# TensorE's table reads stand singly between the gate/up products; the find products move to the last step of four

## The chip, the cores and the metric

The kernel runs on one core of one Trainium2 chip. The metric is the device time of one execution in microseconds (us). Engines are named as in the profile: PE is TensorE's matmul side, PEld its weight loads, DVE VectorE, ACT ScalarE, POOL GpSimd, SP SyncE. A name with a q behind it (PEldq, DVEq, SPq) is that engine's sequencer: the part that reads the instruction stream, works on registers, checks semaphores and hands work to the engine.

## The reference

A state space layer (layer norm, a four-tap convolution, a scan, two projections, residual) is followed by a mixture of experts over 8192 tokens of 512 numbers. Only the second half meets the change:

```python
topk_w, topk_idx = _route(x, w_router, b_router)      # 8 of 64 experts per token
sort = jnp.argsort(idx_flat); tok = sort // TOPK      # (token, expert) pairs by expert
g = jax.lax.ragged_dot(x_sorted, we_gate, group_sizes)   # 512 -> 256
u = jax.lax.ragged_dot(x_sorted, we_up, group_sizes)
o = jax.lax.ragged_dot(jax.nn.silu(g) * u, we_down, group_sizes)   # 256 -> 512
y = jnp.zeros_like(x_flat).at[tok].add(o * w_sorted[:, None])
```

The data type is float32 throughout.

## The kernel before, in words

The stages up to the routing end some 917 us after the span's start. The rest is `expert_tiles`, and only it is touched. It goes over 576 tiles of 128 (token, expert) pairs. 65,536 pairs fill 512 tiles; the other 64 are room for the partly filled last tile of each expert, and those that the routing leaves over stand at the end and carry no token.

A table row in on-chip memory (`k.tiles`, three words a tile) says for each tile which expert it has, whether that expert is new, which of four weight slots it uses, and which earlier tile's result must have been added before its own may be. An engine that needs the word reads it into a register: `entry` is a `value_load`, and `Words.load` keeps the word and its slot number. On every engine these reads have the line 1301 in the profile.

Each product is made of three passes over weights and data split into a high and a low fp32r part. For a tile TensorE does, in this order inside `step(i, s)`:

- `turn_x(i + 1)`: four transposes of the next tile's gathered rows (line 1407), into `ps_x`. It needs `xT_low` of tile i, since the same PSUM tile is used again.
- `find` (line 1420), once in four steps: four small products that compare `past` with the ranks of an expert's tokens, for four tiles that come 12 tiles later. It needs the expert number of each as a register.
- `gate_up(i)`: twelve products of 128x128 by 512 columns (line 1438).
- `turn_h(i - 1)`: two transposes of the hidden row (line 1465).
- `down(i - 2)`: six products (line 1455).

`walk` unrolls the loop eight times, so s runs from 0 to 7; registers don't live across a turn of the loop, so step s = 0 loads the words of tiles i-2, i-1 and i anew. Each later step has the word of its tile from the step before, where `words.load(i + 1, s + 1)` stands right behind the gate/up products. Once in four steps (s of 0 and 4) `experts_of` reads four more entries there, for the four find products of the next step.

VectorE goes over the same tiles in groups of four (`short_walk`). In its step it makes `xT_low` of tile i+1 (`keep_low`, line 1578), splits the weights of a new expert (`split_low`, line 1570: 2.34 us for the gate/up part, 1.23 us for the down part), takes or prepares the find's results, then makes `h` (`hidden`, line 1590), `hT_low` (line 1584) and `y` (`scale`, line 1597). `mark` (line 1602) writes `past`, the comparison that a find multiplies with; `pick` (lines 1609 to 1618) turns two tiles' find results into token numbers, `tile_ids`. ScalarE copies them out seven tiles ahead (`take_ids`, line 1535), and GpSimd gathers the rows five tiles ahead (line 1373). GpSimd also adds the scaled results into the output in memory (line 1381), after SyncE has counted the earlier ones as landed (line 1351); for a tile that carries no token the table asks for all tiles before it.

Of the kernel before, what the change touches and what calls it, by code (L numbers as in the profile page):

```python
# [20 lines left out]
E, F, TOPK = 64, 256, 8  # L21
# [1176 lines left out]
def expert_tiles(nc, k):  # L1198
# [8 lines left out]
    with ExitStack() as ctx:  # L1207
# [92 lines left out]
        def entry(eng, i, field, most):  # L1300
            return eng.value_load(k.tiles[0:1, bass.ds(3 * i + field, 1)], min_val=min(field, 1),  # L1301
                                  max_val=most)
# [95 lines left out]
        @block.tensor  # L1398
        def _(pe):
            words = Words(pe)  # L1400

            def turn_x(i, s):
                pe.wait_ge(gathered[s % XS], 16 // XS * (i - s % XS) + 16)
                after(pe, xT_low_ready, i)
                chunks = x[:, s % XS, 0:D].rearrange("p (q c) -> p c q", c=DC)
                for c in range(DC):
                    last = nc.tensor.transpose(ps_x[:, c, :], chunks[:, c, :], k.ident[:])  # L1407
                last.then_inc(xt_done, 1)

            def experts_of(i):  # L1410
                return [pe.snap(entry(pe, i + t, 0, 2 * WSLOTS * E - 1) // (2 * WSLOTS), min_val=0, max_val=E - 1)
                        for t in range(SHORT)]

            def find(i, experts):


                pe.wait_ge(marked, i + SHORT)
                after(pe, picked, i)
                for t, e in enumerate(experts):
                    last = nc.tensor.matmul(ps_find[t // 2][:, t % 2, :], past[:, t, :],  # L1420
                                            k.ranks[:, bass.ds(e, 1), :].rearrange("j o t -> j (o t)"), start=True,
                                            stop=True)
                    if t % 2 == 1:
                        last.then_inc(found, 2)

            def gate_up(i, s):
                place = words.place(s)
                high, low = (w[:, bass.ds(place, 1), 0:DOWN].rearrange("p o (j c f) -> p c (o j) f", j=2, c=DC)
                             for w in (w_high, w_low))
                pe.wait_ge(w_low_ready[0], i + 1)  # L1430
                pe.wait_ge(xT_high_ready, i + 1)
                after(pe, h_made, i - 1)
                n = 0
                for x, w in ((xT_high, high), (xT_high, low), (xT_low, high)):
                    if x is xT_low:
                        pe.wait_ge(xT_low_ready, i + 1)
                    for c in range(DC):
                        last = nc.tensor.matmul(ps_gu[s % 2][:], x[:, s % 2, c, :], w[:, c], start=(n == 0),  # L1438
                                                stop=(n == 3 * DC - 1))
                        n += 1  # L1440
                last.then_inc(gu_done, 1)

            def down(i, s):
                place = words.place(s)
                high, low = (w[:, bass.ds(place, 1), DOWN:W].rearrange("p o (c d) -> p c (o d)", c=FC)
                             for w in (w_high, w_low))
                pe.wait_ge(w_low_ready[1], i + 2)
                pe.wait_ge(hT_high_ready, i + 1)
                after(pe, y_made, i - 1)
                n = 0  # L1450
                for x, w in ((hT_high, high), (hT_high, low), (hT_low, high)):
                    if x is hT_low:
                        pe.wait_ge(hT_low_ready, i + 1)
                    for c in range(FC):
                        last = nc.tensor.matmul(ps_y[s % 2][:], x[:, s % 2, c, :], w[:, c], start=(n == 0),  # L1455
                                                stop=(n == 3 * FC - 1))
                        n += 1
                last.then_inc(y_done, 1)

            def turn_h(i, s):  # L1460
                pe.wait_ge(h_made, i + 1)
                after(pe, hT_low_ready, i)
                chunks = h[:, s % 2, :].rearrange("p (q c) -> p c q", c=FC)
                for c in range(FC):
                    last = nc.tensor.transpose(ps_h[:, c, :], chunks[:, c, :], k.ident[:])  # L1465
                last.then_inc(ht_done, 1)

            def step(i, s):
                if s == 0:
                    words.load(i - 2, s - 2)  # L1470
                    words.load(i - 1, s - 1)
                    words.load(i, s)
                if exists(i + 1):
                    turn_x(i + 1, (s + 1) % UNROLL)
                if s % SHORT == 1 and exists(i - 1 + AHEAD_FIND):
                    find(i - 1 + AHEAD_FIND, held[0])
                gate_up(i, s)
                if s + 1 < UNROLL:
                    words.load(i + 1, s + 1)
                if s % SHORT == 0 and exists(i + AHEAD_FIND):  # L1480
                    held[0] = experts_of(i + AHEAD_FIND)
                if exists(i - 1):
                    turn_h(i - 1, (s - 1) % UNROLL)
                if exists(i - 2):
                    down(i - 2, (s - 2) % UNROLL)

            held = [None]
            for i in range(0, AHEAD_FIND, SHORT):
                find(i, experts_of(i))
            turn_x(0, 0)  # L1490
            walk(pe, step)
            turn_h(TILES - 1, UNROLL - 1)
            for i in (2, 1):
                down(TILES - i, UNROLL - i)
# [69 lines left out]
        def _(v):  # L1564
# [56 lines left out]
            def step(i, s, slot):  # L1621
                if s == 0:
                    words.load(i, s)
                words.load(i + 1, (s + 1) % SHORT)
                if exists(i + 1):
                    keep_low(i + 1, (s + 1) % SHORT)
                    split_low(i + 1, (s + 1) % SHORT, 0)
                split_low(i, s, 1)
                if s in (1, 2) and exists(i - s + AHEAD_FIND):
                    pick(i - s + AHEAD_FIND, 2 * s - 2)  # L1630
                if s == SHORT - 1 and exists(i + 1 + AHEAD_FIND):
                    mark(i + 1 + AHEAD_FIND)
                hidden(i, s)
                if exists(i - 1):
                    keep_h_low(i - 1, (s - 1) % SHORT)
                if exists(i - 2):
                    scale(i - 2, (s - 2) % SHORT, slot(UNROLL - 2))

            v.sem_inc(w_low_ready[1], 1)
            for i in range(0, AHEAD_FIND, SHORT):  # L1640
                mark(i)
                pick(i, 0)
                pick(i, 2)
            mark(AHEAD_FIND)
            words.load(0, 0)
            split_low(0, 0, 0)
            keep_low(0, 0)
# [90 lines left out]
```

## Time and profile before

| | |
|---|---|
| median of 3 runs | 4089.84 us (4088.28 to 4099.53) |
| profiled execution: its own time | 4088.8 us |
| its span | 4087.0 us, 110080 instructions |
| PE busy | 3666.0 us, 90% |
| PEld / DVE / POOL / ACT busy | 68% / 57% / 39% / 34% |
| mean granted TensorE clock | 0.967 |

The profile is that of one execution. Busy shares are over the whole span, of which the expert tiles take the last 3170 us. A matmul's end is modelled, and matmuls overlap: one of the gate/up products lasts 0.39 to 0.40 us by the profile, while the next starts 0.235 us after it did. "idle" in brackets counts from the modelled end of the last one.

### The profile page before, as it was taken

The numbers are of one execution on the slowest core, as the hardware profiler recorded it, in microseconds if no ns is written. First come the engines' busy times: TensorE is split into PE (matmuls) and PEld (weight loads), VectorE is DVE, ScalarE is ACT, GpSimd is POOL, SyncE is SP. The second block draws the span as 40 slices with busy tenths as digits, with TensorE's granted clock in tenths as the row PEclk, the third lists the DMA queues.
The fourth block names the chain that finished last, engine by engine and source line by source line (L and its number), as shares of the span: only waits on it lengthen the run. The fifth ranks groups of instructions, "written<-read, shape, count | busy, mean of one in ns | idle before, by whom it ended". The sixth has DMA issues, their size and how long they took to land.

```text
span 4087.0 us, 110080 instructions
## 1 busy us (share of the span) xinstructions
PE 3666.0 (90%) x16856; PEld 2789.2 (68%) x16857; DVE 2328.0 (57%) x5809; ACT 1370.5 (34%) x4031; POOL 1603.3 (39%) x1208
## 2 busy tenths in 40 slices
PE   6719999959999999999999999999999999999997
PEld 3305544427777777777777777777777777777775
DVE  5364555555556665656555555555555566555653
ACT  2212222213333333334333333333333333333332
POOL 1100000014445454444444454445444445544443
PEclk9959999979999999999999999999999999999998
DMA  3422222235666665667666666566666566666654
GB/s 112 110 64 91 95 90 95 88 82 106 142 141 131 146 151 115 149 134 162 119 132 122 162 126 136 117 150 129 119 121 135 114 160 150 130 134 149 132 102 76
DMA packets 216177, 502.40 MB, mean 123 GB/s; under 512 B 46587, under 2 KB 46715, under 8 KB 215360
## 3 DMA queue, kind: packets, MB, share of 16 engines
q0 software_dynamic: 129024, 320.94, 41.7%
q1 hardware_dynamic: 86592, 177.77, 13.3%
q10 hardware_dynamic: 512, 3.15, 0.4%
q8 instruction: 17, 0.28, 0.0%
q14 instruction: 32, 0.26, 0.0%
HBM read 1115.65 MB, written 191.41 MB: 320 GB/s over the span
## 4 chain that ended last, share of the span: by engine, by line
PE 68%; issue 5%; DMA 2%; DVE 1%; ACT 1%; DVEq 0%; ACTq 0%; POOLq 0%; POOL 0%; SPq 0%
PE e_ps_gu L1438 38%; PE e_ps_y L1455 19%; PE e_ps_x L1407 6%; PE e_ps_h L1465 4%; DMA out<-e_y,e_y_ids 2%; PE e_ps_find L1420 1%; DVE e_w_low L1570 1%; ACT e_w_high L1507 0%; DVE e_h L1590 0%; ACT e_silu L1526 0%; DMA e_w_raw<-in_L_ffn_we_down 0%; DVE e_below L1613 0%; ACTq L1301 0%; DVEq L1301 0%; DVE e_y L1597 0%
## 5 line engine op out<-in xcount | busy, mean ns | idle before, releaser
L1381 POOL DMA_INDIRECT out<-e_y,e_y_ids x576 | 943.2, 1638 | 1443.2 <-ACT e_weight L1519 827.7
L1373 POOL DMA_INDIRECT e_x<-token_rows,e_x_ids x576 | 609.9, 1059 | 270.8 <-issue 174.5
L1438 PE MATMUL e_ps_gu<-e_w_high,e_xT_high 128*128 x2304 | 680.7, 417 | 1.4 <-DVEq L1573 1.3
L1438 PE MATMUL e_ps_gu<-e_w_high,e_xT_low 128*128 x2304 | 635.2, 397 | 0.0
L1438 PE MATMUL e_ps_gu<-e_w_low,e_xT_high 128*128 x2304 | 633.9, 397 | 0.0
L1597 DVE TENSOR_SCALAR e_y<-e_ps_y,e_weight 128x512 f32 (+1 forms) x576 | 430.5, 747 | 321.6 <-PE e_ps_y L1455 297.1
L1578 DVE TENSOR_TENSOR e_xT_low<-e_ps_x,e_xT_high 128x512 fp32r<-128x512 f32 x576 | 397.8, 691 | 241.3 <-ACT e_xT_high L1515 137.0
L1438 PEld LDWEIGHTS e_ps_gu<-e_w_high,e_xT_low 128*128 128x128 f32 x2304 | 435.5, 189 | 106.8
L1438 PEld LDWEIGHTS e_ps_gu<-e_w_low,e_xT_high 128*128 128x128 f32 x2304 | 433.4, 188 | 103.6
L1526 ACT ACTIVATE e_silu<-e_ps_gu 128x256 f32<-128x256 f32 x576 | 222.0, 385 | 787.3 <-PE e_ps_gu L1438 743.0
L1438 PEld LDWEIGHTS e_ps_gu<-e_w_high,e_xT_high 128*128 128x128 f32 x2304 | 396.1, 192 | 69.5 <-issue 3.1
L1515 ACT CAST e_xT_high<-e_ps_x 128x512 fp32r<-128x512 f32 x576 | 337.2, 585 | 297.5 <-PE e_ps_x L1407 296.3
L1407 PEld LDWEIGHTS e_ps_x<-ident,e_x 128*128 128x128 f32 x2304 | 368.4, 205 | 79.6 <-issue 33.3
L1455 PE MATMUL e_ps_y<-e_w_high,e_hT_high 128*128 x1152 | 417.0, 443 | 0.0
L1590 DVE TENSOR_TENSOR e_h<-e_silu,e_ps_gu 128x256 f32<-128x256 f32 x576 | 241.7, 420 | 275.4 <-ACT e_silu L1526 259.3
L1407 PE MATMUL e_ps_x<-ident,e_x 128*128 128x128 f32 x2304 | 372.0, 284 | 22.9 <-issue 17.5
L1465 PEld LDWEIGHTS e_ps_h<-ident,e_h 128*128 128x128 f32 x1152 | 215.3, 199 | 232.0 <-issue 161.2
L1455 PE MATMUL e_ps_y<-e_w_high,e_hT_low 128*128 x1152 | 368.0, 401 | 0.0
L1455 PE MATMUL e_ps_y<-e_w_low,e_hT_high 128*128 x1152 | 367.0, 400 | 0.0
L1465 PE MATMUL e_ps_h<-ident,e_h 128*128 128x128 f32 x1152 | 238.0, 288 | 137.8 <-issue 107.4
L1535 ACT CAST e_x_ids<-e_tile_ids (+1 forms) x576 | 110.1, 192 | 554.5 <-issue 512.2
L1584 DVE TENSOR_TENSOR e_hT_low<-e_ps_h,e_hT_high 128x256 fp32r<-128x256 f32 x576 | 240.4, 417 | 80.0 <-ACT e_hT_high L1531 79.7
(245 smaller groups left out, 3901.4 us busy)
## 6 DMA issues: line engine op xcount, KB each, us to landing
e_w_raw<-in_L_ffn_we_gate SPq DMA_DIRECT2D x576, 512.0 KB
e_w_raw<-in_L_ffn_we_up SPq DMA_DIRECT2D x576, 512.0 KB
e_w_raw<-in_L_ffn_we_down SPq DMA_DIRECT2D x576, 512.0 KB
a_x<-in_L_attn_x SPq DMA_DIRECT2D x64, 256.0 KB, 3.6
t_x_in<-in_L_attn_x SPq DMA_DIRECT2D x64, 256.0 KB, 2.8
token_rows<-t_xn SPq DMA_DIRECT2D x64, 256.0 KB, 3.0
out<-t_y_out SPq DMA_DIRECT2D x64, 256.0 KB, 2.0
e_x<-token_rows,e_x_ids POOLq DMA_INDIRECT x576
```

What stands on the lines that cost most here:

```text
L1373: pool.indirect_dma_start(x[:, s % XS, :], None, k.rows, bass.IndirectOffsetOnAxis(x_ids[:, s:s + 1], 0)) \
L1381: pool.indirect_dma_start(k.out, bass.IndirectOffsetOnAxis(y_ids[:, s:s + 1], 0), y[:, s % YS, :], None, compute_op=ALU.add).then_inc(adde ...
L1407: last = nc.tensor.transpose(ps_x[:, c, :], chunks[:, c, :], k.ident[:])
L1438: last = nc.tensor.matmul(ps_gu[s % 2][:], x[:, s % 2, c, :], w[:, c], start=(n == 0), stop=(n == 3 * DC - 1))
L1455: last = nc.tensor.matmul(ps_y[s % 2][:], x[:, s % 2, c, :], w[:, c], start=(n == 0), stop=(n == 3 * FC - 1))
L1465: last = nc.tensor.transpose(ps_h[:, c, :], chunks[:, c, :], k.ident[:])
L1515: nc.scalar.copy(xT_high[:, s % 2], ps_x[:]).then_inc(xT_high_ready, 1)
L1526: nc.scalar.activation(silu[:, s % 2, :], ps_gu[s % 2][:, 0, :], ACT.Silu).then_inc(silu_ready, 1)
L1578: nc.vector.tensor_tensor(xT_low[:, s % 2], ps_x[:], xT_high[:, s % 2].bitcast(F32), ALU.subtract).then_inc(xT_low_ready, 1)
L1584: nc.vector.tensor_tensor(hT_low[:, s % 2], ps_h[:], hT_high[:, s % 2].bitcast(F32), ALU.subtract).then_inc(hT_low_ready, 1)
L1590: nc.vector.tensor_tensor(h[:, s % 2, :], silu[:, s % 2, :], ps_gu[s % 2][:, 1, :], ALU.mult).then_inc(h_made, 1)
L1597: nc.vector.tensor_scalar(y[:, bass.ds(slot, 1), :].rearrange("p o d -> p (o d)"), ps_y[s % 2][:], weight[:, s % SHORT:s % SHORT + 1], Non ...
```

## The change

On TensorE, `experts_of`, which read the experts of four tiles in one go, becomes `expert_of` for one tile. The reads move into `gate_up`: after its third, sixth and ninth product `read_ahead` is called with third = 0, 1, 2. The middle place takes the next tile's word. The outer two take, in the steps with s % 4 of 1 and 2, one expert number each (four over the two steps), and in step s = 0 the words of tiles i-2 and i-1. The word of tile i itself is read in step 0 behind `turn_x`. The find products move from steps with s % 4 = 1 to s % 4 = 3, for the same four tiles.

On VectorE `mark` moves from the last step of the group before to the third of the same group, one step ahead of the find. The first `pick` moves from the second step to the fourth, the second one from the third step to the second step of the next group. No product, read or comparison is added or dropped.

```diff
-            def experts_of(i):
-                return [pe.snap(entry(pe, i + t, 0, 2 * WSLOTS * E - 1) // (2 * WSLOTS), min_val=0, max_val=E - 1)
-                        for t in range(SHORT)]
+            def expert_of(i):
+                return pe.snap(entry(pe, i, 0, 2 * WSLOTS * E - 1) // (2 * WSLOTS), min_val=0, max_val=E - 1)
...
                         n += 1
+                        if n in (3, 6, 9):
+                            read_ahead(i, s, n // 3 - 1)
                 last.then_inc(gu_done, 1)
...
+            def read_ahead(i, s, third):
+                if third == 1 and s + 1 < UNROLL:
+                    words.load(i + 1, s + 1)
+                if s == 0 and third == 0:
+                    words.load(i - 2, s - 2)
+                if s == 0 and third == 2:
+                    words.load(i - 1, s - 1)
+                if s % SHORT in (1, 2) and third != 1:
+                    t = 2 * (s % SHORT - 1) + third // 2
+                    if exists(i - s % SHORT + AHEAD_FIND + t):
+                        held[t] = expert_of(i - s % SHORT + AHEAD_FIND + t)
+
             def step(i, s):
-                if s == 0:
-                    words.load(i - 2, s - 2)
-                    words.load(i - 1, s - 1)
-                    words.load(i, s)
                 if exists(i + 1):
                     turn_x(i + 1, (s + 1) % UNROLL)
-                if s % SHORT == 1 and exists(i - 1 + AHEAD_FIND):
-                    find(i - 1 + AHEAD_FIND, held[0])
+                if s == 0:
+                    words.load(i, s)
+                if s % SHORT == SHORT - 1 and exists(i + 1 - SHORT + AHEAD_FIND):
+                    find(i + 1 - SHORT + AHEAD_FIND, held)
                 gate_up(i, s)
-                if s + 1 < UNROLL:
-                    words.load(i + 1, s + 1)
-                if s % SHORT == 0 and exists(i + AHEAD_FIND):
-                    held[0] = experts_of(i + AHEAD_FIND)
...
-                if s in (1, 2) and exists(i - s + AHEAD_FIND):
-                    pick(i - s + AHEAD_FIND, 2 * s - 2)
-                if s == SHORT - 1 and exists(i + 1 + AHEAD_FIND):
-                    mark(i + 1 + AHEAD_FIND)
+                if s == 1 and exists(i - s - SHORT + AHEAD_FIND):
+                    pick(i - s - SHORT + AHEAD_FIND, 2)
+                if s == 2 and exists(i - s + AHEAD_FIND):
+                    mark(i - s + AHEAD_FIND)
+                if s == 3 and exists(i - s + AHEAD_FIND):
+                    pick(i - s + AHEAD_FIND, 0)
                 hidden(i, s)
```

Ahead of the loops the last `pick` and the last `mark` of VectorE's start fall away, since the loop now does them.

## Rows read from the trace of the kernel before

**Rows 1.** The page: slices of the span, and the chain by line.

```profile
PE   6719999959999999999999999999999999999997
...
PEclk9959999979999999999999999999999999999998
...
PE e_ps_gu L1438 38%; PE e_ps_y L1455 19%; PE e_ps_x L1407 6%; PE e_ps_h L1465 4%; DMA out<-e_y,e_y_ids 2%; PE e_ps_find L1420 1%; DVE e_w_low L1570 1%; ACT e_w_high L1507 0%; DVE e_h L1590 0%; ACT e_silu L1526 0%; DMA e_w_raw<-in_L_ffn_we_down 0%; DVE e_below L1613 0%; ACTq L1301 0%; DVEq L1301 0%; DVE e_y L1597 0%
```

**Rows 2.** Two stretches: us, busy time of PE, PEld, DVE, ACT, POOL, clock, DMA.

```profile
917.00:3906.00 2989.00, 2836.57 (x13677) 2301.68 (x13676) 1757.11 (x4094) 1107.28 (x3411) 1468.77 (x1090) 0.99 0.63 135
3906.00:4087.00 181.00, 146.73 (x713) 120.10 (x711) 77.78 (x183) 45.41 (x161) 74.71 (x56) 0.93 0.49 86
```

**Rows 3.** PE in order of time, one step of four reads and the next.

```profile
2405.93 1.10 PE L1438 MATMUL e_ps_gu<-e_w_high,e_xT_low 128*128 x4
2408.01 0.48 PE L1465 MATMUL e_ps_h<-ident,e_h 128*128 128x128 f32 x2 [0.99 <-DVE e_h L1590]
...
2409.95 0.64 PE L1407 MATMUL e_ps_x<-ident,e_x 128*128 128x128 f32 x4
...
2412.82 1.10 PE L1438 MATMUL e_ps_gu<-e_w_high,e_xT_low 128*128 x4
2413.76 0.39 PE L1465 MATMUL e_ps_h<-ident,e_h 128*128 128x128 f32 x2
...
2415.40 0.63 PE L1407 MATMUL e_ps_x<-ident,e_x 128*128 128x128 f32 x4
...
2420.31 0.63 PE L1407 MATMUL e_ps_x<-ident,e_x 128*128 128x128 f32 x4
```

**Rows 4.** Line 1301 (the reads), PE's sequencer, 2403.9 to 2408.0 us.

```profile
L1301 PEldq TENSOR_LOAD <-tiles x5: 296/298/304, 2404.2 to 2407.2; - x5
...
L1301 PEldq SEQ_ASSERT  x5: 18/18/18, 2404.7 to 2407.8; - x5
```

**Rows 5.** The same line where one read stands alone (2419.8 to 2421.2 us), and over 1000 to 3906 us.

```profile
L1301 PEldq TENSOR_LOAD <-tiles x1: 785/785/785, 2420.0 to 2420.0; - x1
...
L1301 PEldq SEQ_ASSERT  x1: 18/18/18, 2421.0 to 2421.0; - x1
...
L1301 PEldq TENSOR_LOAD <-tiles x1195: 295/301/1021, 1000.0 to 3902.8; - x200
```

**Rows 6.** Waits of PE, 917 to 3906 us: us in total, times, longest us.

```profile
PE e_ps_h L1465 <- issue: 106.1, 120, 2.6
PE e_ps_h L1465 <- DVE e_h L1590: 21.2, 13, 2.2
PE e_ps_x L1407 <- issue: 17.5, 17, 1.6
PE e_ps_h L1465 <- DVE e_hT_low L1584: 6.2, 2, 5.2
PE e_ps_x L1407 <- DVE e_xT_low L1578: 5.4, 1, 5.4
```

**Rows 7.** Line 1301 on PE's sequencer right behind the gap of rows 3 (2407.9 to 2412 us).

```profile
L1301 PEldq FUSED_REGOPS  x2: 46/98/151, 2411.0 to 2411.5; - x2
```

**Rows 8.** VectorE in order of time: marks, `xT_low`, and a split.

```profile
2400.63 0.69 DVE L1578 TENSOR_TENSOR e_xT_low<-e_ps_x,e_xT_high 128x512 fp32r<-128x512 f32 x1 [0.80 <-ACT e_xT_high L1515]
...
2401.94 0.68 DVE L1602 TENSOR_TENSOR e_past<-slot_row,begin 64x512 bf16<-64x512 f32 x1 [0.62 <-issue]
...
2416.71 0.69 DVE L1578 TENSOR_TENSOR e_xT_low<-e_ps_x,e_xT_high 128x512 fp32r<-128x512 f32 x1
...
3086.43 2.34 DVE L1570 TENSOR_TENSOR e_w_low<-e_w_raw,e_w_high  x1
```

**Rows 9.** PE's sequencer, line 45 (waits on semaphores), 2417.4 to 2417.6 us.

```profile
L45 PEldq EVENT_SEMAPHORE  x1: 51/51/51, 2417.5 to 2417.5; - x1
```

**Rows 10.** The adds into the output, 3906 to 4087 us.

```profile
L1381 POOL DMA_INDIRECT out<-e_y,e_y_ids x32: 1552/1587/1917, 3906.0 to 4076.3; - x32
...
DMA to landing us min/median/max: 4.4/4.6/5.1
```

More of the change, by code:

```diff
@@ L1485, in step @@
                     down(i - 2, (s - 2) % UNROLL)
-            held = [None]
+            held = [None] * SHORT
             for i in range(0, AHEAD_FIND, SHORT):
-                find(i, experts_of(i))
+                find(i, [expert_of(i + t) for t in range(SHORT)])
             turn_x(0, 0)
@@ L1642, in _ @@
                 pick(i, 0)
-                pick(i, 2)
-            mark(AHEAD_FIND)
+                if i + SHORT < AHEAD_FIND:
+                    pick(i, 2)
             words.load(0, 0)
```

## The prediction

> **What bounds the kernel now.** I read the page first. TensorE is busy in nine tenths or more of nearly every slice from the tenth on, and the chain that ended last is made of its products; the granted clock is at its upper level (2.4 GHz) for that whole stretch [rows 1]. So in the expert stage TensorE sets the pace, and only time in which its array stands idle can be won. The windows split that stage in two [rows 2]: up to 3906 us, and the last 181 us. The last part is a different regime. There GpSimd issues 32 adds into the output from 3906.0 to 4076.3, 170.3 / 31 = 5.49 us apart, each landing 4.6 us after its issue [rows 10]: these are the tiles without tokens, each of which must wait until the one before has landed. That is a chain of transfers that TensorE doesn't hurry. I therefore count nothing won behind 3906 us, and look for the gain in the 2989 us before it.
>
> Next the order of time on PE [rows 3]. Where only one table read stands behind the gate/up products, the transposes of the hidden row start 2413.76 - 2412.82 = 0.94 us after the last group of four products did, with no idle time. Where five reads stand there, it is 2408.01 - 2405.93 = 2.08 us. The profile names `e_h` as what ended that wait. I don't believe the name: the sequencer's own rows [rows 4] show the five reads at 2404.2 to 2407.2, the last assertion belonging to them at 2407.8, and the transpose starts 0.2 us after that. The array had run dry while its sequencer was still reading. One read costs the sequencer (2407.2 - 2404.2) / 4 = 0.75 us, five of them 3.75 us. The first was begun at 2404.2, when the array was only at the first of the twelve products (the last group of four begins at 2405.93, eight products of 0.94 / 4 = 0.235 us earlier is 2404.05): the sequencer was a lead of some 2.9 us ahead, and 3.75 us spend it.
>
> **The sum.** PE's waits over this stretch [rows 6] are 106.1 + 21.2 + 6.2 = 133.5 us in front of `e_ps_h` (135 times) and 17.5 + 5.4 = 22.9 us in front of `e_ps_x` (18 times; there the three word reads of step s = 0 and the loop's branch stand). These are idle times from the modelled end. From start to start a gap is worth more: the shown one is 2.08 - 0.94 = 1.14 us against 0.99 idle, so 0.15 more. Behind it the array starts anew: from the transposes to the next `turn_x` it takes 2409.95 - 2408.01 = 1.94 us against 2415.40 - 2413.76 = 1.64 us. That 0.30 us is the largest such case that I saw; I take 0.20 for the mean. So the gaps are worth 133.5 + 135 x 0.35 = 180.8 us and 22.9 + 18 x 0.25 = 27.4 us, together 208 us.
>
> A check from another side: an ungapped step is 2420.31 - 2415.40 = 4.91 us, and a step with the find takes 2415.40 - 2409.95 = 5.45 us, so four tiles take 20.18 us when nothing stands idle, 5.05 us each. 544 tiles would take 2747 us where 2989 us are used: 242 us is the most that could be won if every stall of every sort went. The 208 us lie inside that.
>
> **Part by part.** *The five reads of one step become 1, 3, 3 and 1.* Their number stays: 18 in eight steps. What counts is whether the array still runs dry. Let T be the time at which the sequencer passes the wait for `xT_low` ahead of `turn_x`. It is the wait that stops it in an ordinary step: `xT_low` ends at 2417.40 [rows 8] and the sequencer's wait passes at 2417.5 [rows 9], while `turn_x` runs on the array at 2420.31 [rows 3], 2.9 us later. The sequencer needs, without reads, at most 2411.0 - 2407.8 = 3.2 us for a whole step that has a find in it [rows 4, 7], so for an ordinary one about 2.4 us (an estimate: the find's register work and products off). Of that I put 1.2 us between T and the end of gate/up, by its share of twelve in 24 pairs of weight load and product. With three reads the last three products are issued at about T + 1.2 + 3 x 0.75 = T + 3.5. The array wants them at T + 2.9 + 0.47 (transposes) + 9 x 0.235 = T + 5.5. 2 us remain. The whole step costs the sequencer 2.4 + 2.25 = 4.7 us, less than the array's 4.91, so two of these steps in a row don't eat the lead. Step s = 0 has four reads: T + 4.3 against T + 5.5, and 5.4 us for the step, so it hands on 0.5 us of delay, which the next step has room for. Over eight steps the sequencer has 18 x 0.75 + 8 x 2.4 + 2 x 0.8 (finds) = 34 us of work against 40.4 us of the array. The reads are therefore costed at nothing; the cover is the queue of products, and if it were gone each would cost up to 0.75 us.
>
> A read that stands alone lasts longer: 0.785 us for the load itself instead of 0.30, and 1.02 at most; the median over 1195 is 0.301 [rows 5]. With three such reads a step would cost 3 x 1.24 + 2.4 = 6.1 us; this is a rival below.
>
> *The words of step 0 move behind `turn_x` and into the products.* The three reads and the branch that stood ahead of `turn_x` go: the 27.4 us are in the sum.
>
> *Find and mark.* The find needs `past`. It used to be marked nearly two steps before; now it is one. A mark ends at 2402.62, 1.30 us after the `xT_low` of its step at 2401.32 [rows 8], and the array comes to the find 2.9 + 0.5 = 3.4 us after that `xT_low`. 2.1 us are spare, so in ordinary steps the wait is hidden. Where a new expert's gate/up weights are split ahead of the mark (2.34 us and some 0.3 us around it) it is late by 0.5 us and by what VectorE is behind already. Of 64 experts a quarter begins at such a tile: 16 x 1 us, say 15 us lost, between 0 and 30. Behind it in the sequencer's stream stand the gate/up products.
>
> *Pick.* The same instructions, moved. Token numbers come 2 to 3 steps later; `take_ids` still has about two steps. VectorE is busy 1757 of 2989 us [rows 2]. Nothing.
>
> *What does not go.* Of the waits, the two that are over 5 us (5.2 and 5.4) are too long for reads alone; at that place late weights stand behind them. I leave 8 us. A shorter cycle also gives VectorE, ScalarE and the weight transfers less time around a new expert: 3 us.
>
> Together 208 - 15 - 8 - 3 = 182 us. The profiled execution took 4088.8 us, its span is 4087.0, and the median is 4089.84, 1 us above it: 4089.8 - 182 = 3908 us, 4.4% less.
>
> **One rule weighed.** In the trace the sequencer's lead is at most about 17 pairs of weight load and product: the lone read at 2420.0 [rows 5] starts just ahead of the last down product, with four transposes and twelve gate/up products to come. The Trainium skill (TensorE: Matmul & The Clock Gate, the paragraph on engine queue depths) gives TensorE a queue of 64. By that number the lead could be 32 pairs, over 5 us of work, the five reads would be covered already, and moving them would be worth nothing. The trace disagrees: the gap is there, and it ends with the last read. I give it a rival's place all the same.
>
> **Rivals.**
> - *Long reads.* If reads inside the products take 1.24 us as the lone one did, a step of three costs 6.1 us against 4.91, two in a row lose 2.4 us, and about 1.4 us of slack takes half of it: some 0.7 to 1 us per four tiles, 136 x 0.75 = 100 us back. 3908 + 100 = 4008, with recoveries 3980 us. For it: rows 5; against: the median, and that the lone reads stood where the sequencer had nothing to hurry for.
> - *Another engine takes over.* VectorE or ScalarE, behind after a split, or the adds at a change of expert (5.49 us from one to the next against a new pace of 5.05) hold TensorE. About half of the gain goes: 3995 us. Against: in the steps without five reads no wait of PE appears in the list.
> - *No gain.* The gaps are not the reads' but what the profile names (`e_h`), as also by the skill's queue: 4090 us. Against: the sequencer's times.
> - *The other side.* A read between products stops the array, since it would wait for what has been issued. It decides from 208 / 1195 = 0.17 us a read; at the load's own 0.30 us it costs 358 us: 4090 - 208 + 358 = 4240 us. Against: reads today run beside products without a gap.
>
> **How the numbers follow.** Forecast 65% (own range 3875 to 3940), long reads 14%, another engine 12%, no gain 4%, the other side 5%. What a measurement of this kernel can tell from no change is about 0.3%, 12 us. Faster: 65 + 14 + 12 = 91%; the same 4%; slower 5%. The range reaches from 3870 (the 242 us less 22) to 3990, which leaves out some two in ten.
>
> **What would show it.** Right: no idle time before `e_ps_h` and `e_ps_x` beyond some 15 us; the adds of the tail beginning near 3725 us and still 5.5 us apart; a step of 4.91 us with the find at 5.45. The mark's price would show as a wait in front of `e_ps_find`. Wrong: idle time inside the twelve products at every fourth step (long reads), waits for `e_h`, `e_hT_low` or weights in any step (another engine), or a prolonged product line with a read behind each third one.

## The result, and the profile after

The changed kernel takes 3975.55 us (median of 4 runs, 3973.47 to 3986.54) against 4090.98 us for the kernel before (median of 4 runs, three of which are those of the table above); the ratio is 0.9721 with a 95% interval of 0.9707 to 0.9735. That is 115 us less, where 182 us were forecast. The time lies inside the stated range of 3870 to 3990 us, but outside the forecast's own range of 3875 to 3940 us, and some two thirds of the gain came.

The page of the changed kernel, the same slices as in [rows 1]:

```profile
PE   6809999967999999999999999999999999999996
...
PEclk9959999988999999999999999999999999999998
```

Two stretches, as in [rows 2]: the stage up to the first add of the tail, and the tail. The columns are us, busy time of PE, PEld, DVE, ACT and POOL, granted clock, DMA share and GB/s.

```profile
917.00:3789.00 2872.00, 2821.04 (x13672) 2286.70 (x13673) 1744.54 (x4089) 1087.36 (x3412) 1468.24 (x1089) 1.00 0.66 140
3789.00:3972.00 183.00, 146.30 (x717) 120.88 (x715) 77.68 (x188) 45.00 (x161) 75.15 (x56) 0.92 0.49 85
```

The first stretch is 2872 us where it was 2989, so all of the gain lies there. The tail keeps its length, as its adds say (3789 to 3972 us, compare [rows 10]): (3961.0 - 3789.3) / 31 = 5.54 us from one to the next.

```profile
L1381 POOL DMA_INDIRECT out<-e_y,e_y_ids x32: 1552/1586/2082, 3789.3 to 3961.0; - x32
```

What PE waited for in the first stretch (us in total, times, longest), to be held against [rows 6]:

```profile
PE e_ps_find L1419 <- DVE e_past L1611: 24.1, 32, 2.7
PE e_ps_gu L1437 <- issue: 10.0, 48, 0.6
PE e_ps_x L1407 <- DVE e_xT_low L1587: 6.8, 3, 6.1
PE e_ps_gu L1437 <- DVEq L1582: 4.1, 7, 1.7
PE e_ps_h L1466 <- DVE e_hT_low L1593: 2.9, 1, 2.9
```

The waits in front of `e_ps_h` and `e_ps_x` were 156.4 us in 153 places and are 9.7 us in 4. So the old gaps are gone. Two new kinds stand in their place: the find products wait for the mark, and 48 gaps have opened between the gate/up products.

Both can be seen around one new expert. VectorE of the changed kernel, in order of time:

```profile
1086.07 2.29 DVE L1579 TENSOR_TENSOR e_w_low<-e_w_raw,e_w_high  x1
...
1091.56 0.69 DVE L1587 TENSOR_TENSOR e_xT_low<-e_ps_x,e_xT_high 128x512 fp32r<-128x512 f32 x1
1092.97 1.23 DVE L1579 TENSOR_TENSOR e_w_low<-e_w_raw,e_w_high  x1 [0.72 <-ACTq L1518]
...
1094.41 0.71 DVE L1611 TENSOR_TENSOR e_past<-slot_row,begin 64x512 bf16<-64x512 f32 x1 [0.21 <-issue]
```

And PE, there and in an ordinary find step:

```profile
1094.23 0.63 PE L1407 MATMUL e_ps_x<-ident,e_x 128*128 128x128 f32 x4
1095.32 0.72 PE L1419 MATMUL e_ps_find<-ranks,e_past 64*128 x4 [0.46 <-DVE e_past L1611]
1096.14 1.20 PE L1437 MATMUL e_ps_gu<-e_w_high,e_xT_high 128*128 x4
...
1158.66 0.63 PE L1407 MATMUL e_ps_x<-ident,e_x 128*128 128x128 f32 x4
1159.22 0.40 PE L1419 MATMUL e_ps_find<-ranks,e_past 64*128 x4
1159.55 1.20 PE L1437 MATMUL e_ps_gu<-e_w_high,e_xT_high 128*128 x4
```

The mark ends at 1095.12, and the find starts 0.2 us after it. From `turn_x` to the first gate/up product it takes 1.91 us there, 0.89 us in the ordinary step: this late mark costs 1.0 us, of which the idle time of 0.46 us shows less than half. The rest is the restart, in which I take it that the sequencer has no lead and hands on the finds and the first products as it makes their addresses: the finds and what follows them start 0.82 us apart in place of 0.33. What stands ahead of the mark is not only the split of the gate/up part, but that of the down part (1.23 us) in the step behind it. Going by the starts of all products, 34 finds were late, 45 us in all: 16 behind a gate/up split (1.5 us each in the mean), 17 behind a down split (1.05 us each), and one behind both. Where a step was ordinary, none was.

### The profile page after: what moved, and what is told of

It is laid out like the page before. It is cut to its first block, busy times and chain, and to the rows that moved or that the text cites. A ratio compares the mean times of both kernels' runs of the same rounds, so it can differ in the third digit from the quotient of the medians.

```text
span 3971.7 us, 110141 instructions
## 1 busy us (share of the span) xinstructions
PE 3650.4 (92%) x16856; PEld 2774.8 (70%) x16857; DVE 2313.6 (58%) x5802; ACT 1349.9 (34%) x4031; POOL 1602.0 (40%) x1208
## 4 chain that ended last, share of the span: by engine, by line
PE 59%; DVE 5%; issue 5%; DVEq 2%; ACT 2%; DMA 2%; ACTq 1%; POOLq 0%; POOL 0%; SPq 0%
PE e_ps_gu L1437 34%; PE e_ps_y L1456 16%; PE e_ps_x L1407 5%; DVE e_w_low L1579 3%; PE e_ps_h L1466 3%; ACT e_w_high L1516 2%; DMA out<-e_y,e_y_ids 2%; PE e_ps_find L1419 1%; DVEq L1301 1%; ACTq L1301 1%; DVE e_past L1611 1%; DVE e_y L1606 1%; DVE e_below L1622 0%; DVEq L1579 0%; ACT e_silu L1535 0%
## 5 line engine op out<-in xcount | busy, mean ns | idle before, releaser
L1437 PE MATMUL e_ps_gu<-e_w_low,e_xT_high 128*128 x2304 | 646.6, 399 | 6.4 <-issue 4.8
L1437 PE MATMUL e_ps_gu<-e_w_high,e_xT_low 128*128 x2304 | 650.4, 401 | 0.2 <-issue 0.2
L1466 PEld LDWEIGHTS e_ps_h<-ident,e_h 128*128 128x128 f32 x1152 | 226.4, 197 | 51.7 <-DVE e_h L1599 3.4
L1456 PEld LDWEIGHTS e_ps_y<-e_w_high,e_hT_low 128*128 128x128 f32 x1152 | 218.2, 189 | 51.1
L1579 DVE TENSOR_TENSOR e_w_low<-e_w_raw,e_w_high x128 | 225.4, 1761 | 48.7 <-ACTq L1518 25.0
```

What stands on the lines that cost most here:

```text
L1579: split_weights(v, words, s, lambda half, place: nc.vector.tensor_tensor(w_low[:, bass.ds(place, 1), PARTS[part]], w_raw[:, bass.ds(half, ...
```

## The experiments

The kernel before was run again beside them, with medians of 4090.28 us (runs 1 to 4), 4094.43 us (5 to 7) and 4094.05 us (8 and 9); each ratio is against that one.

**1. The table words are read behind `xT_low`, not ahead of it.** In the median `xT_low` of the first step of four ended only 1.8 us ahead of the next `turn_x`, in place of 2.9. The reason seemed to be that ScalarE and VectorE read two words at the head of a group. On ScalarE the copy of `xT_high` becomes a function of its own, `keep_xT`, and moves ahead of the reads together with `take_ids`; on VectorE `keep_low` moves ahead of them.

```diff
+                if exists(i + AHEAD_IDS):
+                    take_ids(i + AHEAD_IDS, slot(AHEAD_IDS))
+                if exists(i + 1):
+                    keep_xT(i + 1, (s + 1) % SHORT)
                 if s == 0:
                     words.load(i + 1, s + 1)
                 words.load(i + 2, (s + 2) % SHORT)
-                if exists(i + AHEAD_IDS):
-                    take_ids(i + AHEAD_IDS, slot(AHEAD_IDS))
...
+                if exists(i + 1):
+                    keep_low(i + 1, (s + 1) % SHORT)
                 if s == 0:
                     words.load(i, s)
                 words.load(i + 1, (s + 1) % SHORT)
                 if exists(i + 1):
-                    keep_low(i + 1, (s + 1) % SHORT)
```

> The changed kernel, but ScalarE copies xT_high and VectorE makes xT_low before they read the table words of their step, not behind. Theory A (what is left of TensorE's idle time inside the twelve products comes from xT_low arriving late ahead of the steps with three reads: 1.8 us ahead of turn_x in the median instead of 2.9): xT_low comes 0.7 to 1 us earlier in the first step of four, the idle time inside the products (some 55 us from start to start) falls to under 20, and the time is 3930 to 3945 us. Rival B (the reads that last 0.5 us and more do it, wherever xT_low stands): no change, 3970 to 3980 us.

Measured: 3994.13 us, ratio 0.9763 (0.9747 to 0.9779), so 18 us slower than the changed kernel. Its waits of PE (917 to 3812 us):

```profile
PE e_ps_find L1419 <- DVE e_past L1616: 24.4, 33, 2.7
PE e_ps_gu L1437 <- DVEq L1587: 18.0, 28, 1.2
PE e_ps_gu L1437 <- issue: 15.0, 62, 0.8
```

Theory A falls. The edit did what it was meant to do: `xT_low` of the first step of four now ends 2.9 us ahead of the next `turn_x` in the median. But the gaps between the products did not shrink (15.0 us of idle time where they were 10.0). The rival's time was missed too. What the edit did is in the second row: the word now stands between `xT_low` and the split, the split comes later, and the products wait for the low weights 28 times. So `xT_low` is not the lever, and late low weights of a new expert cost time. Whether longer reads do, this run can't say, since it left them as they were.

**2. The mark two steps ahead.** `past` gets two halves, which the finds read in turn, and VectorE marks at the end of the first step of four.

```diff
-        past = sb("past", [NB, SHORT, P], BF16)
+        past = sb("past", [NB, 2 * SHORT, P], BF16)
...
-                if s == 2 and exists(i - s + AHEAD_FIND):
-                    mark(i - s + AHEAD_FIND)
...
                     scale(i - 2, (s - 2) % SHORT, slot(UNROLL - 2))
+                if s == 0 and exists(i + AHEAD_FIND):
+                    mark(i + AHEAD_FIND, slot(0))
```

> The changed kernel, but past has two halves and VectorE marks at the end of the first step of four, two steps ahead of the find in place of one. If the wait for the mark costs what the trace shows (34 late finds, some 44 us from start to start with what stands behind them), the time is 3930 to 3945 us and no wait for e_past is left. Rival: VectorE is simply late around a new expert, and the wait only moves to xT_low, w_low or h of the same step: 3965 to 3980 us.

Measured: 3942.21 us, ratio 0.9636 (0.962 to 0.9652). No wait for `e_past` is left (917 to 3762 us):

```profile
PE e_ps_gu L1437 <- issue: 10.9, 51, 0.6
PE e_ps_gu L1437 <- DVEq L1582: 9.2, 21, 0.9
PE e_ps_h L1466 <- DVE e_hT_low L1593: 8.6, 2, 7.8
PE e_ps_x L1407 <- DVE e_xT_low L1587: 4.8, 2, 4.4
```

3975.6 - 3942.2 = 33 us came back. The time is in the expected window, but the 44 us that were named with it did not all come: part of it moved to the low weights (idle time from 4.1 to 9.2 us) and into the gate/up products.

**3. Reads in lumps, find and takes as changed.** An edit of the changed kernel: `read_ahead` falls away, and the four expert numbers are read behind the products of the step ahead of the find.

```diff
-                        if n in (3, 6, 9):
-                            read_ahead(i, s, n // 3 - 1)
...
+            def step(i, s):
+                if s == 0:
                     words.load(i - 2, s - 2)
...
                     words.load(i - 1, s - 1)
...
+                    words.load(i, s)
...
                 gate_up(i, s)
+                if s + 1 < UNROLL:
+                    words.load(i + 1, s + 1)
+                if s % SHORT == 2 and exists(i - 2 + AHEAD_FIND):
+                    held[:] = [expert_of(i - 2 + AHEAD_FIND + t) for t in range(SHORT)]
```

> The find, the mark and the takes stand as in the changed kernel, but TensorE's reads are in lumps as before: the four expert numbers behind the gate/up products of the third step, the next tile's word behind every step's products, three words at the head of step 0. Theory: the gain is all from the spreading, so this is about the kernel before, 4080 to 4110 us (the wait for the mark hides behind the lump), with idle time before e_ps_h of 110 to 150 us. Rival: the move of the find alone brings part of the gain: under 4060 us.

Measured: 4061.95 us, ratio 0.9937 (0.9921 to 0.9954), 28 us less than before and 18 us below the forecast of the theory; it lies at the rival's edge, not past it. The gaps are back in front of `e_ps_h` (917 to 3876 us):

```profile
PE e_ps_h L1464 <- issue: 117.5, 135, 2.0
PE e_ps_h L1464 <- DVE e_hT_low L1583: 4.5, 2, 4.0
...
PE e_ps_x L1407 <- issue: 2.8, 8, 0.6
```

That is 122 us where [rows 6] have 133.5. The 17.5 us in front of `e_ps_x` fell to 2.8; the lump of four no longer falls into the step that begins with three words, but no run takes that apart from the move of find, mark and takes. So of the 115 us some 28 come with these moves and with where the four reads stand, and the rest, 86 us net, from the spreading of the reads.

**4. Only the words move between the products.** The four expert reads stay behind the products of steps 0 and 4, find and VectorE as before.

```diff
+                        if n in (3, 6, 9):
+                            read_ahead(i, s, n // 3 - 1)
...
+            def read_ahead(i, s, third):
+                if third == 1 and s + 1 < UNROLL:
+                    words.load(i + 1, s + 1)
+                if s == 0 and third == 0:
+                    words.load(i - 2, s - 2)
+                if s == 0 and third == 2:
+                    words.load(i - 1, s - 1)
...
-                if s == 0:
-                    words.load(i - 2, s - 2)
-                    words.load(i - 1, s - 1)
-                    words.load(i, s)
                 if exists(i + 1):
                     turn_x(i + 1, (s + 1) % UNROLL)
+                if s == 0:
+                    words.load(i, s)
...
                 gate_up(i, s)
-                if s + 1 < UNROLL:
-                    words.load(i + 1, s + 1)
                 if s % SHORT == 0 and exists(i + AHEAD_FIND):
                     held[0] = experts_of(i + AHEAD_FIND)
```

> The kernel before, with only the word reads put singly between the products; the four expert reads stay in a lump in steps 0 and 4, the find and VectorE stay as they were. Theory (what counts is how many reads stand between the wait for xT_low and the next transposes, not where they stand): step 0 now has eight reads in that stretch in place of five, its gap grows by 0.5 to 0.8 us, while the 27 us ahead of turn_x go: 4085 to 4120 us. Rival (single reads between products are hidden as such): 27 us and part of the gaps go, under 4050 us.

Measured: 4195.47 us, ratio 1.0253 (1.0233 to 1.0272), 105 us slower than before. The direction is that of the theory, the size is not. PE around one step 0:

```profile
2498.38 0.63 PE L1407 MATMUL e_ps_x<-ident,e_x 128*128 128x128 f32 x4
...
2500.72 1.10 PE L1438 MATMUL e_ps_gu<-e_w_high,e_xT_low 128*128 x4
2503.88 0.48 PE L1467 MATMUL e_ps_h<-ident,e_h 128*128 128x128 f32 x2 [2.07 <-issue]
...
2505.85 1.05 PE L1457 MATMUL e_ps_y<-e_w_high,e_hT_low 128*128 x2
2506.70 1.05 PE L1407 MATMUL e_ps_x<-ident,e_x 128*128 128x128 f32 x4
```

and the window with it:

```profile
2100.00:2500.00 400.00, 373.24 (x1751) 299.23 (x1751) 228.02 (x527) 142.50 (x439) 191.64 (x140) 0.96 0.61 130
```

Eight reads between two waits cost 8 x 0.75 = 6 us, against some 6.2 us from the wait for `xT_low` to the transposes of the hidden row (2.9 + 0.4 + 2.9 us), which must also hold the sequencer's other work; the gap is 2.07 us. Then four transposes last 1.05 us where they last 0.63: TensorE's clock has fallen to the lower of its levels (1.2 instead of 2.4 GHz), and the granted clock of the window is 0.96. Over tiles 3 to 540 the trace has 178 us at the lower level, where the kernel before has 48. So the 105 us have two parts. The stretch from the last gate/up product to the transposes is 205 us over the ungapped one in all, in place of 155, 50 us more. Half of the 130 us more at the lower level, 65 us as an estimate from above, is time lost in slow products; what had stood ahead of `turn_x` is gone in return. The expectation had only the gaps. Three of the eight reads had stood at the head of the step, ahead of the wait for `xT_low`; as I read it, the sequencer would mostly have waited there anyway, and a read moved out of a waiting time costs its full price.

**5. The outer reads in the down products.** The two expert numbers of a step (in step 0 the word of tile i-1) are read behind the second and the fourth down product of the step; the rest stays as in the changed kernel.

```diff
             def down(i, s, ahead=None):
...
                         n += 1
+                        if ahead and n in (2, 4):
+                            read_between(*ahead, n // 2 - 1)
```

> The changed kernel, but the outer two of the three places for reads move from the gate/up products (behind the third and the ninth) to the down products of the same step (behind the second and the fourth); the next tile's word stays behind the sixth gate/up product, and in step 0 the word of tile i-2 behind the third. Theory C (the gaps inside the gate/up products open only where a new expert's split has held the sequencer at the head of the products, so that it has no lead and three reads between twelve products cost more time than the products): the gaps of 0.3 us and more inside them go, 25 to 45 us off, 3930 to 3955 us. Rival B (the reads as such stop the array, or long ones do): the gaps move to the down products and the time stays at 3970 to 3980 us.

Measured: 3971.21 us, ratio 0.9699 (0.9678 to 0.9721), 4 us less than the changed kernel, which the scatter of the runs hardly tells from nothing. It is outside the window of theory C, and inside the rival's. Its waits (917 to 3793 us):

```profile
PE e_ps_find L1419 <- DVE e_past L1618: 34.2, 34, 3.1
...
PE e_ps_y L1456 <- issue: 4.2, 22, 0.2
...
PE e_ps_gu L1437 <- issue: 0.6, 3, 0.3
```

The gaps between the gate/up products are gone (10.0 to 0.6 us), 4.2 us came in the down products, and the wait for the mark grew from 24.1 to 34.2 us: TensorE arrives at the find sooner, and VectorE's mark is no earlier. From start to start the down products cost more than their idle time shows, 20 us where they cost 1 (table in the next section), so the rival is right that part of the price moves there. And products were slow behind late marks:

```profile
1097.41 0.70 PE L1419 MATMUL e_ps_find<-ranks,e_past 64*128 x4 [0.85 <-DVE e_past L1618]
1098.23 2.02 PE L1437 MATMUL e_ps_gu<-e_w_high,e_xT_high 128*128 x4
```

These four gate/up products last 2.02 us where they last 1.20 at the upper level. The trace has 41 us at the lower level, that of the changed kernel 7: up to 17 us that hide a gain in this execution.

**6. Both.** The edits of 2 and 5.

> The early mark with two halves of past, and the reads in the down products, together. If the two costs are separate, as theory C has it: 3942 less 25 to 45, so 3897 to 3920 us. If they share one cause (VectorE late around a new expert): 3935 to 3945 us, no better than the early mark alone.

Measured: 3921.8 us, ratio 0.9577 (0.9555 to 0.96). That is 20 us less than the early mark alone, and 54 us less than the changed kernel; 2 us above the window of theory C and clear of the rival's. With the mark out of the way the move of the reads shows what it is worth. In this pair the clock plays no part: both traces have 14 us at the lower level. Waits, 917 to 3739 us:

```profile
PE e_ps_gu L1437 <- DVEq L1589: 11.2, 25, 0.9
PE e_ps_h L1468 <- DVE e_hT_low L1600: 8.0, 2, 7.2
PE e_ps_x L1407 <- DVE e_xT_low L1594: 5.0, 2, 4.6
PE e_ps_y L1456 <- issue: 5.0, 26, 0.2
```

**7. One read more in the steps with three.** An edit of the changed kernel.

```diff
                 if third == 1 and s + 1 < UNROLL:
                     words.load(i + 1, s + 1)
+                if s % SHORT in (1, 2) and third == 1:
+                    words.load(i + 1, s + 1)
```

> The changed kernel with one more read of the same word behind the sixth product in the steps that have three (four there, 280 more reads in all). Theory C: in ordinary steps the lead still covers nearly all of it, since the sequencer then needs 2.4 + 3.0 = 5.4 us in two steps running and catches up in the next two; with a new expert it adds its 0.75 us where it falls: 3990 to 4020 us. Rival: there is no lead left in the three-read steps, each added read costs its 0.75 us: 280 x 0.75 = 210 us, 4150 us and more.

Measured: 4022.72 us, ratio 0.983 (0.9804 to 0.9855), 47 us more for some 280 reads, 3 us above theory C's window and far below the rival's time. That is 0.17 us a read, net, where 0.75 would be the uncovered price. The waits (917 to 3840 us) are now

```profile
PE e_ps_gu L1437 <- issue: 41.8, 96, 1.1
PE e_ps_find L1419 <- DVE e_past L1613: 6.5, 9, 2.0
```

TensorE comes later to the find, so the mark costs less (idle time 6.5 in place of 24.1 us). From the first to the last of the twelve gate/up products the stage is 124 us over the ungapped time where it was 49: the reads themselves cost 75 / 280 = 0.27 us each. There is a lead left in ordinary steps, but three reads are near its end: in 34 of 76 ordinary steps with s of 2 or 6 (the second in a row with four reads) the products took over 0.25 us too long.

**8. One edit of the kernel before: the next word in the middle.**

```diff
                         n += 1
+                        if n == 6 and s + 1 < UNROLL:
+                            words.load(i + 1, s + 1)
...
                 gate_up(i, s)
-                if s + 1 < UNROLL:
-                    words.load(i + 1, s + 1)
```

> The kernel before with one edit: the next tile's word is read behind the sixth gate/up product, not behind the twelfth. The four expert reads stay in a lump behind the products in steps 0 and 4, the three words at the head of step 0. Theory D (a lump behind the products is covered only by what is queued then, some 2.9 us; a read in the middle is taken while the sequencer would stand before a full queue anyway): four reads of 0.75 us are covered in step 4, its gaps go, some 70 us with the restarts; in step 0 the sequencer comes late from its three words and the gap stays: 4010 to 4030 us. Rival (only the number of reads between the wait for xT_low and the transposes counts): no change, 4085 to 4095 us.

Measured: 4073.18 us, ratio 0.9949 (0.9932 to 0.9965). The sign is theory D's, the size (21 us) is less than a third of it, and the time is in neither window. Waits, 917 to 3900 us:

```profile
PE e_ps_h L1467 <- issue: 84.0, 78, 2.3
PE e_ps_h L1467 <- DVE e_h L1590: 27.7, 17, 2.0
```

With five more for `e_hT_low` that is 100 idle places in front of `e_ps_h` where there were 135. The starts of the products say which: all 67 gaps in steps 0 stayed, and 28 of 66 in steps 4. Of these 28, 27 stand where the tile of the step or one of the two before it is the first of a new expert (27 such steps in all), and one among the 41 others. So the edit closes the gap in ordinary steps, and a lead already lost to a new expert keeps it open. The size was off also because a gap in step 4 is smaller than one in step 0: from the first gate/up product to the transposes it is 3.59 us in the median before, in step 0 4.01, without a gap 2.89.

**9. Five reads singly, but within one step.** The kernel before, with find and takes as they were.

```diff
+                        if n == 6 and s + 1 < UNROLL:
+                            words.load(i + 1, s + 1)
+                        if s % SHORT == 0 and n in (2, 4, 8, 10) and exists(i + AHEAD_FIND):
+                            held[(2, 4, 8, 10).index(n)] = expert_of(i + AHEAD_FIND + (2, 4, 8, 10).index(n))
```

> The kernel before, with the four expert reads and the word put singly between the gate/up products of the same step (behind the 2nd, 4th, 6th, 8th and 10th); find, mark and takes as before, the three words at the head of step 0 too. Theory D: step 4 loses its gap as in the run beside it; in step 0 the sequencer has nearly no lead, so five reads still cost about 1 us there, now between the products: 4000 to 4030 us. Rival E (single reads are hidden wherever they stand, the lump is what costs): step 0 loses its gap too, 3930 to 3960 us.

Measured: 4101.28 us, ratio 1.0021 (1.0012 to 1.0031): no gain at all, a little slower. PE in one step 0:

```profile
2411.97 0.72 PE L1437 MATMUL e_ps_gu<-e_w_high,e_xT_high 128*128 x2
2413.10 0.73 PE L1437 MATMUL e_ps_gu<-e_w_high,e_xT_high 128*128 x2 [0.42 <-issue]
2414.14 0.70 PE L1437 MATMUL e_ps_gu<-e_w_low,e_xT_high 128*128 x2 [0.30 <-issue]
2415.11 0.71 PE L1437 MATMUL e_ps_gu<-e_w_low,e_xT_high 128*128 x2 [0.28 <-issue]
2416.00 1.52 PE L1437 MATMUL e_ps_gu<-e_w_high,e_xT_low 128*128 x4 [0.18 <-issue]
2417.36 0.39 PE L1468 MATMUL e_ps_h<-ident,e_h 128*128 128x128 f32 x2
```

One gap of 1 us has become four or five small ones, and together they cost more than it did. From the first gate/up product to the transposes this step takes 5.39 us; the median of the 67 steps 0 is 5.04 us, where the kernel before has 4.01, and 0.28 us more until the down products. Rival E is out: reads aren't hidden by standing singly. Theory D's gain in step 4 did come (a median of 2.89 us where it was 3.59; 27 of 68 are still late, again those around a new expert), but step 0 lost it again: its five reads cost 2.1 us and not the 1 us that the theory gave them.

## Why the prediction was right, and where it was off

*What bounds the kernel.* Right. TensorE set the pace, the tail kept its 5.5 us from add to add, and the gain ended at its head (3906.0 to 3789.3 us). One reading of [rows 1] was too coarse: the clock was not at its upper level for the whole stretch. The trace of the kernel before has 48 us of the stage at the lower level (tiles 3 to 540), that of the changed one 7. The sum has no term for it.

*The gap is the reads', whatever name the profile gives.* Right. The 21.2 us put down to `e_h` went with the rest, though nothing about `e_h` was made faster; run 3, with the reads in a lump again, brought the gaps back in its own step. The rivals of no gain and of the other side are out, and so is the queue that covers the reads. By that rule (the Trainium skill, "TensorE: Matmul & The Clock Gate", the paragraph on engine queue depths) the five reads would have been covered; the trace had the gap, and the change removed it. That does not measure the queue's length: the sequencer's lead is cut in each step by the wait for `xT_low`, and the trace shows only how far it got, some 17 pairs.

*The account of the stage.* The waits list only idle time from modelled ends. The starts of the products give the whole. For tiles 3 to 540 the table has each part's time over that of an ungapped step (0.39 us from `turn_x` to the first gate/up product and 0.89 with a find between; 2.89 and 2.92 to the transposes of the hidden row; 0.15 to the down products; 1.49 to the next `turn_x`), summed, in us:

| | before | changed | run 2 | run 3 | run 5 | run 6 |
|---|---|---|---|---|---|---|
| `turn_x` to gate/up, with find | 8 | 45 | 0 | 16 | 54 | 2 |
| `turn_x` to gate/up, other steps | 2 | 12 | 17 | 12 | 12 | 19 |
| gate/up to the transposes | 155 | 51 | 61 | 145 | 24 | 18 |
| transposes to down | 24 | -1 | -1 | 11 | -1 | -1 |
| down to the next `turn_x` | 34 | 1 | 2 | 12 | 20 | 19 |
| sum | 222 | 107 | 78 | 196 | 109 | 56 |

222 - 107 = 115 us is the gain between the two profiled executions, and all of it.

*The gross sum of 208 us.* From the last gate/up product to the transposes it was 155 us and is 3; with the two rows below that, 213 us became 3: 210 us went. The agreement is partly luck. The waits fell by 156.4 - 9.7 = 147 us, which with the sum's own additions for 149 gaps (some 50 us) makes 197; the 210 also hold products slowed by the clock, at most half of 48 us, which the sum did not have.

*The terms taken off it were too small.* They were 26 us and came out at 210 - 115 = 95 us:

- **The mark: 15 us forecast, 37 us more in the steps with a find (45 in place of 8).** "Of 64 experts a quarter begins at such a tile" counts only the split of the gate/up part; the down part is split one step later, and that too stands ahead of the mark. Twice as many finds were late, 34 and not 16, and a late one cost 1.3 us in the mean and not 1. Run 2 takes the mark away, and 33 us come back.
- **The reads: "costed at nothing", 48 us.** From the first to the last of the twelve gate/up products the stage was 1 us over the ungapped time and is 49 us; run 3, with the same find and marks but no read between the products, has 4 us. The budget was made for ordinary steps, and there it held: 49 of the 51 us from gate/up to the transposes stand in the 181 steps whose tile, or one of the two before it, is the first of a new expert. There the sequencer is held at the head of the gate/up products by the low weights, and starts with no lead: of the new experts' own tiles that fall into a step with three reads, 26 have their first product 0.27 us behind the end of the split, and the twelve products of each take 1.06 us too long or more. In run 2 four such tiles fall into a step with one read, with the product 0.6 us or less behind the split, and none takes longer. Reads moved out of these products take some 42 us with them (run 6 against run 2), but cost 19 us between the down products, so that 20 us are left as a gain. The lead I had taken, 2.9 us, is 1.8 us in the median in the first step of four; run 1 brought it back to 2.9, and showed that this was not the lever.
- **The low weights and the rest: 9 us more from `turn_x` to gate/up in the other steps,** where 11 us had been set aside for what stays and for a new expert's shorter time.

*Where the number lies.* 3976 us is inside the stated range only because that goes on to 3990 us, which takes in the rival of the long reads (3980 us). By the forecast's own sum that is luck. The forecast's own range ended at 3940 us. The time is thus near the two rivals that take some half of the gain, and the cost that came was one that the forecast had at 15 us and one that it had at nothing. Two signs of being wrong showed up in part: idle time inside the twelve products, though not at every fourth step, and waits for the low weights.

*Another engine takes over* was a rival at 12% with the whole gain halved (3995 us). Its mechanism is most of what happened: VectorE's splits around a new expert hold TensorE at the find and at the low weights for 45 + 12 of the 107 us that are left, and they take the lead without which the reads cost the other 50. It is not apart from the forecast as I had drawn it. *Long reads* was right that three reads can be too many, but for the wrong cause: reads did not get longer. From 1000 to 3700 us 185 of 1158 loads on TensorE's sequencer lasted over 0.5 us, before it was 189 of 1110. And its step from 4008 to 3980 us has no working behind it.

## What to carry to other kernels

Count what an engine's sequencer has to do between two of its waits, and compare it with the array's work in that stretch: reads of 0.75 us each are free up to that sum in a step that begins with a lead, not in one where the sequencer was held up just before, and one that stood in a waiting time is not free any more once moved out of it. Spreading helps by the number of reads in a stretch, not by their standing singly: two of the nine edits (4 and 9) put reads singly into a stretch that had no room, and were slower or no better. When a sum of idle times is too small for the time that changed, add up the starts of the products, step by step. And when a wait is moved closer to what it waits for, count every piece of work ahead of it on the other engine, in its rare steps, not in the ordinary one.

## What the runs showed of the hardware that I had not expected

A short gap can be enough to bring TensorE's clock to its lower level. PE in the kernel before, and below it the window with its granted clock, 0.50:

```profile
1132.57 0.47 PE L1465 MATMUL e_ps_h<-ident,e_h 128*128 128x128 f32 x2 [2.08 <-DVE e_h L1590]
...
1134.01 1.05 PE L1455 MATMUL e_ps_y<-e_w_low,e_hT_high 128*128 x2
```

```profile
1133.00:1136.00 3.00, 3.00 (x9) 2.31 (x9) 0.42 (x1) 0.56 (x2) 0.00 (x0) 0.50 0.55 142
```

The down products last 1.05 us where they last 0.63. In this trace 12 of 13 falls of the clock stand just behind an idle time of over 1.5 us on PE (there are 28 such), none behind the 44 of 0.8 to 1.5 us. In run 4 it is 44 of 48 falls, with 70 such gaps, and the stage's granted clock is 0.97 (917 to 4010 us). But in run 5 seven falls stand behind waits of 0.84 to 1.26 us, so the length of the one gap does not settle it, and what does, no run shows. Taking the gaps away gave back the clock too: 48 us at the lower level before, 7 in the changed kernel.

A restart costs more than its idle time shows: 0.46 us of idle time at a late mark goes with 1.0 us from start to start, and 0.99 us in front of `e_ps_h` with 1.44 us [rows 3]. And the cause that is named for an idle time can be any event that happened nearby: `e_h` was named for 13 gaps, and they went with the reads.
